# An attention layer on one core: when the third maxima are issued and which bank holds the second half of the keys

## What is computed

```python
# x (16, 512, 32, 32): 16 images, 512 channels, n = 1024 pixels; all float32
qkv = jnp.einsum('bchw,oc->bohw', x, w_qkv)           # 1536 x 512 weights
q, k, v = jnp.split(qkv, 3, axis=1)                   # 8 heads of 64 rows, q scaled by 1/8
sim = jnp.einsum('bhdi,bhdj->bhij', q, k)
attn = jax.nn.softmax(sim, axis=-1)
out = jnp.einsum('bhij,bhdj->bhid', attn, v)
y = jnp.einsum('bchw,oc->bohw', out, w_out) + b_out
y = y * jax.lax.rsqrt(mean_sq + SCALE) * rms_scale    # mean_sq over the 512 channels
return y + x
```

## Time and profile before

| what | us |
|---|---|
| median of three runs | 3962.96 |
| the three runs | 3962.96, 3962.63, 3970.72 |
| the profiled execution | 3978.09 |
| its span, first to last instruction | 3976.0 |
| PE busy | 3911.9 (98%) |
| PEld busy | 2460.2 (62%) |
| POOL busy | 2966.9 (75%) |
| DVE busy | 2803.0 (70%) |
| ACT busy | 2313.7 (58%) |

### The profile page before, as it was taken

The page is one execution under the profiler, slowest core; times in us unless marked ns, Lnnn a source line. Parts: engine busy times, 40 slices in busy tenths (PEclk is TensorE's granted clock), DMA queues, the critical chain, the costliest instruction groups (busy, mean ns, idle before and its releaser), DMA issues.

```text
span 3976.0 us, 53150 instructions
## 1 busy us (share of the span) xinstructions
PE 3911.9 (98%) x18630; PEld 2460.2 (62%) x18630; DVE 2803.0 (70%) x2899; ACT 2313.7 (58%) x4048; POOL 2966.9 (75%) x2332
## 2 busy tenths in 40 slices
PE   8999999999999999999999999999999999999997
PEld 5666666656666666665666666666665666666663
DVE  6667676676766767677686776767667676676775
ACT  4556565555655656565565665655556556565654
POOL 5678777776877778777787777877777777787776
PEclk9999999999999999999999999999999999999998
DMA  3111111111111201102011020111111111111100
GB/s 149 49 47 54 43 67 51 43 54 43 67 51 43 74 22 70 58 33 75 27 67 56 35 72 32 64 54 38 69 54 43 54 38 69 54 51 45 63 33 22
DMA packets 71847, 212.18 MB, mean 53 GB/s; under 512 B 8216, under 2 KB 9368, under 8 KB 58784
## 3 DMA queue, kind: packets, MB, share of 16 engines
q1 hardware_dynamic: 71584, 208.80, 14.7%
HBM read 168.92 MB, written 39.85 MB: 53 GB/s over the span
## 4 chain that ended last, share of the span: by engine, by line
PE 96%; DVE 1%; issue 1%; ACT 0%; DMA 0%; POOL 0%; SPq 0%; ACTq 0%; DVEq 0%; POOLq 0%
PE pv L729 24%; PE aux L549 17%; PE score L707 13%; PE score L716 12%; PE aux L587 9%; PE aux L616 9%; PE aux L692 7%; PE pv L648 3%; PE aux L673 2%; ACT probs L816 0%; DVE inv_sum L1098 0%; DVE k_l L1033 0%; PE aux L601 0%; DVE maxima L1040 0%; PE aux L626 0%
## 5 line engine op out<-in xcount | busy, mean ns | idle before, releaser
L1211 POOL TENSOR_TENSOR prob_sum<-prob_sum,probs 128x512 f32<-128x512 f32 x1536 | 1964.6, 1308 | 356.6 <-ACT probs L816 356.6
L816 ACT ACTIVATE probs<-score 128x512 f32<-128x512 f32 x2048 | 1111.0, 595 | 783.8 <-PE score L716 777.3
L1040 DVE TENSOR_REDUCE maxima<-aux 128x1 fp32r<-128x1024 f32 x768 | 914.0, 1218 | 416.1 <-PE aux L692 269.8
L729 PE MATMUL pv<-probs,v_sb 128*64 128x512 f32 x4096 | 998.1, 608 | 0.0
L707 PE MATMUL score<-q_hl,k_hh 128*128 128x512 f32 x2048 | 841.8, 411 | 9.1 <-ACT probs L816 9.1
L716 PE MATMUL score<-q_hm,k_l 72*128 72x512 f32 x2048 | 814.7, 398 | 0.5 <-DVE q_hm L1058 0.5
L549 PE MATMUL aux<-x_hi,w_ring 128*128 128x512 f32 x2048 | 654.6, 397 | 10.2 <-DMA scale_sb<-scale 9.3
L1207 POOL TENSOR_TENSOR prob_sum<-probs 128x512 f32<-128x512 f32 x256 | 325.1, 1292 | 393.7 <-ACT probs L816 391.6
L729 PEld LDWEIGHTS pv<-probs,v_sb 128*64 128x64 f32 x4096 | 249.6, 136 | 483.4 <-issue 475.6
L707 PEld LDWEIGHTS score<-q_hl,k_hh 128*128 128x128 f32 x2048 | 387.5, 189 | 179.4 <-issue 87.0
L549 PEld LDWEIGHTS aux<-x_hi,w_ring 128*128 128x128 f32 x2048 | 387.3, 189 | 97.6 <-DMA scale_sb<-scale 9.3
(11 more groups left out here) (114 smaller groups left out, 5123.6 us busy)
## 6 DMA issues: line engine op xcount, KB each, us to landing
w_ring<-w_split SPq DMA_DIRECT2D x93, 1024.0 KB, 4.8
stage<-x SPq DMA_DIRECT2D x252, 256.0 KB, 4.6
out<-stage SPq DMA_DIRECT2D x124, 256.0 KB, 2.0
w_split<-w_ring SPq DMA_DIRECT2D x3, 1024.0 KB, 12.3
w_split<-y_sb SPq DMA_DIRECT2D x3, 1024.0 KB, 3.8
y_sb<-wqkv SPq DMA_DIRECT2D x4, 512.0 KB, 8.5
probs<-wqkv SPq DMA_DIRECT2D x2, 512.0 KB, 7.2
probs<-wout SPq DMA_DIRECT2D x1, 1024.0 KB, 8.2
```

What stands on the lines that cost most here:

```text
L729: pe.matmul(pv[half][e * D:(e + 1) * D, :], v_sb[:, pair // 2, j, (pair % 2) * P + e * D:(pair % 2) * P + (e + 1) * D], probs[:, (b * SLOT ...
L816: act.activation(probs[:, step % RING, e, :], score[e][:], ACT.Exp, scale=SOFT).then_inc(prob_ready, 1)
L1040: dve.tensor_reduce(maxima[:, n:n + 1], bank(k, 2), AX_X, ALU.max).then_inc(aux_free[k], 1)
L1211: pool.tensor_tensor(prob_sum[:, e, :], prob_sum[:, e, :], probs[:, step % RING, e, :], ALU.add).then_inc(prob_added, 1)
```

## The change

```diff
-VALUES_FIRST = (2, 1, 2, 1, 2, 1, 2, 1)
+VALUES_FIRST = (2, 1, 1, 1, 1, 1, 2, 1)
@@ def items_at(slot, t, first, last):
     if t == 7:
         if slot in (0, 2, 4):
-            out.append(("K1", 1))
+            out.append(("K1", 1 if slot == 0 else 3))
@@ claim_beside
                 other, n = beside_counts(body.plan, body.b, (slot, name))
-                if body.plan is not pro and pro.end[other] or body.plan is pro and n > 0:
+                if n > 0:
                     pe.wait_ge(aux_free[other], n)
@@ item, PE
                 elif name[0] == "K":
                     kpair, h = (slot // 2 + 1) % PAIRS, int(name[1])
-                    k = body.at(slot, name)[0] if part == 1 else claim(body, slot, name)
+                    k, _ = body.at(slot, name)
+                    if part != 1:
+
+                        claim(body, slot, name, two=k == 3)
```

## The result

| what | us |
|---|---|
| changed kernel, median of 22 executions | 3993.33 (3959.71 to 4021.56) |
| kernel before, median of 22 | 3964.95 (3953.87 to 3995.18) |
| ratio | 1.0056, 95% interval 1.0033 to 1.0078 |
| predicted | 3966 (3956 to 3975) |
| profiled execution, its span | 4015.34, 4013.3 |

What follows compares the result with a forecast made beforehand. PE's own stream, 96% of the chain, was taken as the bound. Against the median with one stall: slot 2 +3.9, batch 0 -0.1, slot 4 -1.3, stall growth +0.5, giving +3.0 us, 3966.0; range 3956 to 3975.

Steps and rivals of the forecast that it cites:

- The new wait: Slot 2, place 9: M21 waits for K1's subtraction on DVE, stretch 5.86 in place of 5.58, 0.28 us worse.
- Slot 4, 5.50: Slot 4, place 9: M21 ties with K1's end, hands over 0.10 late; stretch 5.50 in place of 5.58.
- The direct term: Slots 2 and 4 without stalls, against the median: 14 x 0.28 = +3.9, batch 0 -0.1, slot 4 -1.3.
- the 0.08 of slot 4: Slot 4, place 9: 0.08 us better in each of 16 batches, -1.3 us.
- The added waits: M00, M11, M21, M31 and O1's second half, 5 x 127 places: nothing to 6 us, taken as nothing.
- The starved slots: Slot 2: L1111 on DVE held up by POOL, 7.98 us in place of 1.84; chance unchanged, one stall in the median.
- the second rival: Place 4 of slot 2: another starved L1111 in the median execution, 3966.0 + 8.1 = 3974; chance 0.28.
- A starved slot's own growth: Slot 2 when stalled: one more value behind the wait, 0.86 less 0.33, some 0.5 us each.
- One POOL operation and no more: L1111 on DVE: by the skill's port rule it waits for one POOL operation; 1.84 agrees, 7.98 does not.

Runs made afterwards that it cites:

- k1_bank3: The kernel before with K1 of slots 2 and 4 in bank 3 and all added waits, M2 not moved earlier; median 3975.61, ratio 1.0001.
- waits_once: The changed kernel with waits on bank 3 kept only where K1 can be outstanding, the 635 others removed; median 3981.51, ratio 1.0023 against the kernel before.
- the second set: L1111 moved to place 2 (changed kernel 3958.01, kernel before 3958.46) or a two-element DVE write in front of it (3959.31, 3954.95); no changed-kernel control.
- the third: Changed kernel as control, 3968.61; two-element write before L1111 in changed kernel 3962.57, in kernel before 3966.96; L1111 at place 2 in kernel before 3958.00.

## Why the prediction was wrong

- **The new wait** held as a mechanism. "M21 starts at 1341.90, 0.36 late", stretch 5.86: measured 5.86, with the two errors of 0.04 that cancel (above). That its weights were not loaded ahead is in the trace: in slot 3 of batch 5 the weight load of M31 starts at 1375.24, 0.23 ahead of its matmuls, in slot 2 at 1345.02, together with them. Slot 4, 5.50: measured 5.55 to 5.56, since the pair started 0.06 late (673.50, 0.39 behind M20) and handed over 0.11 late, where I had 0.00 and 0.10; and of the 0.03 gained nothing reached the length of the slot. Slot 2 grew by 0.33, not 0.28, and slot 3 lost 0.05. The direct term was 14 x 0.28 - 0.1 - 1.3 = +2.5; it is 15 x 0.3 = +4.5, 1.3 of the difference for the 0.08 of slot 4 that did not come.
- **The added waits** cost nothing that shows, as taken: slots 0, 1, 5, 6 and 7 kept their lengths to 0.02, and `k1_bank3` and `waits_once` show the same.
- **The starved slots** were the failed step: "Nothing ahead of L1111 changes in slot 2, so I expect the chance of a stall to stay", and with it one stall in the median. In the comparison there were 4.3 against 1.8, by the estimate from the means. In the medians it is (3993.33 - 3959) / 8.1 = 4.2 where I had one: about 26 of the 27 us by which I missed. This is the second rival, "slower, by one more stall", by two and a half in place of one. That nothing ahead of L1111 changes was nearly true: it came at 15.98 to 16.00 from the slot's start in both kernels, POOL's second addition at 15.98 to 16.00 before and 15.96 to 15.99 after. But such a distance doesn't tell the starved from the others (batches 9 and 12 above), and why there were more stays open. I had three executions, whose two levels I read as one and two stalls, and made of them a term for the median with a spread of one. The 22 showed 0 to 5 for the same kernel. The range should have been wider for it, upwards above all: the number can't fall below none.
- **A starved slot's own growth**, 0.5: 38.41 to 38.98 against 37.79 to 38.58, 0.3 in the mean of seven and of three.
- **One POOL operation and no more.** This I had read out of the Trainium skill (SBUF — State Buffer, "Who interferes with whom"), by which the one that issues first has the shared ports for its whole instruction. In 195 of the 225 cases at place 4 it was so. In 30 the waiting VectorE instruction was passed by five further POOL operations, all of which started after it; there the measurement decides against first come, first served.
- **The range** would have held two of the three other medians of the changed kernel: 3968.61 and 3962.95 (ratios 1.0017 and 0.9995), not 3984.63 (1.0035). So whether this forecast hits depends on the set, and a hit would have been luck.

What is shown: that the time beyond the +4.5 is, to some 3 us, starved L1111 at place 4 of slot 2 (counted in the profiles, inferred from the times elsewhere; with the instruction at place 2 there are 0 in 75 in the profiles, and no 8 us step in 57 executions). What stays open: what sets their number. It differs by set, and so by chip or time (one or two in 33 executions in the second), and by execution; that the change as such raises it is neither shown nor excluded. Several comparisons on one chip, and one on several chips at a time, would have been the run to make.

## What to carry to other kernels

When several runs of one kernel lie at levels a constant step apart, find the step in the trace (here one instruction of 7.96 us in place of 1.82) before costing anything smaller, and take its number as a draw, not as a constant of the kernel. A VectorE instruction with two inputs in SBUF, behind which PE's next wait hangs, is a risk where it comes early in a POOL operation with others queued behind. Here it helped to move it to where less than 0.2 us of a POOL operation was left; look in the trace for how much is left when it starts, and put a control on the same chip beside each attempt to cure it, since the second set looked like a cure until the third had one.

## What the runs showed of the hardware

- A scaling by DVE with two SBUF inputs takes 0.74 to 0.75 us where 0.17 to 0.20 us are left of the POOL operation at work, and 1.8 us where the whole addition is ahead of it; it then ends some 0.55 behind POOL's. No row here shows it with POOL idle. It took 7.88 to 7.98 where five more POOL operations followed the one at work without a gap (358.23 to 365.64, 7.4 us): at place 4, once passed over, it was passed over each time until POOL itself stopped, in 30 of 30.
- A POOL addition ahead of which it was let in is 0.44 longer (5.47 in place of 5.03 for the four).
- At place 10, where POOL stops after the next addition, it loses one more at most: 2.5 to 3.0 us, in 74 of 300.
- The distance to the start of POOL's operation does not decide it: with 0.030 us in both, batch 9 of the changed kernel's profile was starved and batch 12 let in. With less than 0.6 us left of that operation none of 419 was passed over.
- A stall of PE of 6.4 us cost 7.9 in the slot (38.41 against 30.51), the rest because PE ran part of what followed at 1.2 GHz (granted clock 0.91 of the slot; the twelve values behind M21 took 4.29 us in place of 2.79); the 6 us stalls of before cost 7.6 to 8.4.
